# LayerNorm of the incoming unit and of the finished unit computed together, over both tiles

## What is computed

```python
x = x + _L0_conv_ref(_ln_c(x), ...)     # _ln_c: (v - mean) / sqrt(var + 1e-06), over the 512 channels
t = _to_tokens(x)
t = t + _L0_ffn_ref(_ln_t(t), ...)      # _ln_t: the same with 1e-05; the ffn replaces tokens 1..128
x = _from_tokens(t, x)
```

## Time and profile before

| | us |
|---|---|
| median of three runs | 1304.27 |
| lowest and highest | 1303.02, 1305.35 |
| profiled execution | 1302.34 |
| its span | 1300.6 |
| PE busy (matmuls) | 1100.8 (85%) |
| DVE busy | 1157.0 (89%) |
| ACT busy | 806.6 (62%) |
| POOL busy | 1110.7 (85%) |

### The profile page before, as it was taken

How to read it: one execution, slowest core, us unless ns; L and a number is a source line. 1 busy time by engine, 2 the same in 40 slices (tenths; PEclk the granted TensorE clock), 3 DMA queues, 4 the chain that set the end, 5 groups by cost and what they waited for, 6 DMA issues and landing times.

```text
span 1300.6 us, 13356 instructions
## 1 busy us (share of the span) xinstructions
PE 1100.8 (85%) x3818; PEld 660.8 (51%) x3818; DVE 1157.0 (89%) x1345; ACT 806.6 (62%) x1496; POOL 1110.7 (85%) x747
## 2 busy tenths in 40 slices
PE   6588888888888988988988988988988888887997
PEld 4344554544544544544544544545545545444887
DVE  1399999999999999999999999999999999999751
ACT  2476765766766666766666666666757657656230
POOL 4299899898898898898898898898998998988750
PEclk8789999999999898898998998999998998998998
DMA  6221321222221221221222212213212213215351
GB/s 160 75 96 53 104 97 58 87 94 77 80 98 68 92 99 57 99 99 61 98 82 78 99 64 96 99 57 104 99 56 104 99 56 116 96 63 168 115 159 30
DMA packets 64539, 116.80 MB, mean 90 GB/s; under 512 B 34218, under 2 KB 47954, under 8 KB 64466
## 3 DMA queue, kind: packets, MB, share of 16 engines
q1 hardware_dynamic: 64466, 115.96, 26.3%
HBM read 108.47 MB, written 7.47 MB: 89 GB/s over the span
## 4 chain that ended last, share of the span: by engine, by line
POOL 29%; PE 22%; DVE 21%; issue 21%; ACT 6%; POOLq 0%; SPq 0%; DVEq 0%; DMA 0%; ACTq 0%
POOL SCAN L413 16%; DVE SCAN L967 13%; PE Yp L693 8%; POOL SCAN L425 6%; DVE SCAN L922 4%; PE PP L772 3%; PE PP L839 3%; PE PP L722 2%; PE PP L819 2%; POOL XN L450 1%; PE PP L812 1%; POOL GATES L418 1%; DVE GATES L951 1%; ACT SGZ L598 1%; POOL XN L441 1%
## 5 line engine op out<-in xcount | busy, mean ns | idle before, releaser
L967 DVE TENSOR_TENSOR_SCAN SCAN<-DA,CAR,SCAN 128x384 f32<-128x384 f32 x768 | 729.8, 1000 | 38.4 <-POOL SCAN L425 36.5
L413 POOL TENSOR_TENSOR SCAN<-SCAN,CS 128x768 f32<-128x768 f32 x384 | 693.9, 1821 | 27.2 <-DVE SCAN L967 26.8
L490 ACT ACTIVATE DA<-UDT,A 128x384 f32<-128x384 f32 x768 | 441.8, 581 | 389.6 <-DVE SCAN L967 386.3
L693 PE MATMUL Yp<-SCAN,IDENT 128*128 128x384 f32 x1536 | 593.7, 512 | 97.5 <-POOL SCAN L413 89.6
L693 PEld LDWEIGHTS Yp<-SCAN,IDENT 128*128 128x128 f32 x1536 | 289.7, 198 | 304.9 <-POOL SCAN L413 143.5
L922 DVE TENSOR_TENSOR SCAN<-UDT,BB 128x768 f32<-128x768 f32 x288 | 268.7, 933 | 11.1 <-PE BB L675 9.2
L425 POOL TENSOR_TENSOR SCAN<-UDT,BS 128x768 f32<-128x768 f32 x96 | 175.4, 1827 | 0.0
L839 PE MATMUL PP<-XN,WT 128*128 128x384 f32 x384 | 139.8, 499 | 0.0
L839 PEld LDWEIGHTS PP<-XN,WT 128*128 128x128 f32 x384 | 75.8, 199 | 56.6 <-issue 11.8
L445 POOL TENSOR_TENSOR UDT<-UDT 128x768 f32<-128x768 f32 x24 | 43.5, 1811 | 69.9 <-DVE UDT L1056 69.9
L675 PE MATMUL BB<-PT,SEL 96*128 96x384 bf16 x288 | 98.3, 342 | 4.6 <-DVE SCAN L922 4.6
(11 more groups left out here) (161 smaller groups left out, 1155.4 us busy)
## 6 DMA issues: line engine op xcount, KB each, us to landing
CS<-bc_rows SPq DMA_DIRECT2D x96, 768.0 KB, 4.0
BS<-bc_rows SPq DMA_DIRECT2D x24, 768.0 KB, 6.0
out<-XN SPq DMA_DIRECT2D x32, 192.0 KB, 2.4
X<-in_x SPq DMA_DIRECT2D x24, 192.0 KB, 3.6
X<-in_L_ffn_memory_tokens SPq DMA_DIRECT2D x16, 256.0 KB, 3.0
XN<-in_L_ffn_memory_tokens SPq DMA_DIRECT2D x16, 256.0 KB, 3.1
bc_rows<-XDT SPq DMA_DIRECT2D x24, 48.0 KB, 1.5
X<-in_L_ffn_memory_router SPq DMA_DIRECT2D x1, 512.0 KB, 3.8
```

The lines of the kernel that those rows point to most:

```text
L413: pool.tensor_tensor(M[:, n1 % MRING], HB[:, n1 % HRING], over_halves(CS[:, n1 % CRING]), ALU.mult).then_inc(m_ready, 1)
L490: act.activation(DA[:, h, 0:T], DT[:, par, h], ACT.Exp, scale=A[:, h, n:n + 1])\
L693: last = pe.matmul(Yp[:, h, 0:T], IDENT[:, :], M[:, n3 % MRING, h], start=n3 == 0, stop=n3 == NS - 1)
L967: dve.tensor_tensor_scan(HB[:, s % HRING, h], DA[:, h, 0:T], HB[:, s % HRING, h], CAR[:, ds(J * NS * HALVES + s * HALVES + h, 1)], ALU.mul ...
```

## The change

`XC`, `SQ`, `LNV` and `RSTD` get a further dimension of two: index 0 is the finished unit, index 1 the incoming one. Where both exist, the mean is 4 matmuls of 192 columns over both tiles of `X` (four units apart), with the result in one bank; the subtraction, the square and the exponential are one instruction each over both. The two logarithms stay apart, since their added constants differ. POOL's instructions stay as they are, but L437 now waits for the common exponential. Where only one norm exists, the code does what it did. The pairs of semaphores become one each. The block for the mean of the finished unit now stands behind the router's matmuls in the queue, and these get a wait of their own.

```diff
-        XC = sb("XC", [P, Q, TOK]); SQ = sb("SQ", [P, Q, TOK])
-        LNV = sb("LNV", [P, TOK]); RSTD = sb("RSTD", [P, TOK])
-        XC2 = sb("XC2", [P, Q, TOK]); SQ2 = sb("SQ2", [P, Q, TOK])
-        LNV2 = sb("LNV2", [P, TOK]); RSTD2 = sb("RSTD2", [P, TOK])
+        XC = sb("XC", [P, 2, Q, TOK]); SQ = sb("SQ", [P, 2, Q, TOK])
+        LNV = sb("LNV", [P, 2, TOK]); RSTD = sb("RSTD", [P, 2, TOK])
...
-        small = SQ[:, :, :].rearrange("p q t -> p (q t)")
+        small = SQ[:, 1].rearrange("p q t -> p (q t)")
...
-        SCO = XC[0:BATCH, :, :].rearrange("p q t -> p (q t)")[:, 0:MEM]
+        SCO = XC[0:BATCH, 1].rearrange("p q t -> p (q t)")[:, 0:MEM]
...
-        STAT = PP[:, 1, 0:TOK]; STAT2 = PP[:, 0, 0:TOK]
...
+        def norms(back, norm):
+            return slice(0 if back else 1, 2 if norm else 1)
+        def norm_x(J, back, norm):
+            units = [J - 1] * back + [J + 3] * norm
+            if len(units) == 1:
+                return unit_x(units[0]).unsqueeze(1)
+            return X[:, :].rearrange("p (u q t) -> p u q t", u=UNITS, q=Q)[:, units[0]:units[1] + 1:4]
+        def norm_stat(back, norm):
+            bank = PP[:, 1 if norm else 0]
+            return bank[:, 0:(back + norm) * TOK].rearrange("p (i t) -> p i t", t=TOK)
...
                 if back and s == 13:
-                    pool.wait_ge(rstd2_ready, k + 1)
-                    pool.tensor_tensor(XC2[:, :, :], XC2[:, :, :], over_q(RSTD2[:, :]), ALU.mult)\
+                    pool.wait_ge(rstd_ready, J + 4)
+                    pool.tensor_tensor(XC[:, 0], XC[:, 0], over_q(RSTD[:, 0]), ALU.mult)\
                         .then_inc(xh2_done, 1)
...
-                    pool.wait_ge(rstd_ready, g + 1)
+                    pool.wait_ge(rstd_ready, J + 4)
                     for r1 in range(2):
-                        pool.tensor_tensor(seq_rows(unit_seq(g), r1), by_row_parity(XC[:, :, :], r1),
-                                           by_row_parity(over_q(RSTD[:, :]), r1), ALU.mult).then_inc(xn_part, 1)
+                        pool.tensor_tensor(seq_rows(unit_seq(g), r1), by_row_parity(XC[:, 1], r1),
+                                           by_row_parity(over_q(RSTD[:, 1]), r1), ALU.mult).then_inc(xn_part, 1)
...
-                if back and s == 11:
-                    act.wait_ge(xc2_ready, k + 1)
-                    act.activation(SQ2[:, :, :], XC2[:, :, :], ACT.Square).then_inc(sq2_ready, 1)
-                if back and s == 12:
-                    act.wait_ge(var2_ready, k + 1)
-                    act.activation(LNV2[:, :], STAT2, ACT.Ln, bias=EPST[:, 0:1]).then_inc(ln2_done, 1)
-                    act.wait_ge(ln2_done, k + 1)
-                    positive(act, out_ready, k)
-                    act.activation(RSTD2[:, :], LNV2[:, :], ACT.Exp, scale=-0.5).then_inc(rstd2_ready, 1)
+                if (back or norm) and s == 11:
+                    i = norms(back, norm)
+                    act.wait_ge(xc_ready, J + 4)
+                    positive(act, var_ready, J + 3)
+                    act.activation(SQ[:, i], XC[:, i], ACT.Square).then_inc(sq_ready, 1)
+                if (back or norm) and s == 12:
+                    i = norms(back, norm)
+                    stat = norm_stat(back, norm)
+                    act.wait_ge(var_ready, J + 4)
+                    if back:
+                        act.activation(LNV[:, 0], stat[:, 0], ACT.Ln, bias=EPST[:, 0:1]).then_inc(ln_done, 1 + (not norm))
+                    if norm:
+                        act.activation(LNV[:, 1], stat[:, back + norm - 1], ACT.Ln, bias=EPSC[:, 0:1]).then_inc(ln_done, 1 + (not back))
+                    act.wait_ge(ln_done, 2 * (J + 4))
+                    if back:
+                        positive(act, xh2_done, k)
+                    if norm:
+                        positive(act, xn_ready, g)
+                    act.activation(RSTD[:, i], LNV[:, i], ACT.Exp, scale=-0.5).then_inc(rstd_ready, 1)
...
-                if norm and s == 11:
-                    act.wait_ge(xc_ready, g + 1)
-                    positive(act, var_ready, g)
-                    act.activation(SQ[:, :, :], XC[:, :, :], ACT.Square).then_inc(sq_ready, 1)
-                if norm and s == 12:
-                    act.wait_ge(var_ready, g + 1)
-                    act.activation(LNV[:, :], STAT, ACT.Ln, bias=EPSC[:, 0:1]).then_inc(ln_done, 1)
-                    act.wait_ge(ln_done, g + 1)
-                    positive(act, xn_ready, g)
-                    act.activation(RSTD[:, :], LNV[:, :], ACT.Exp, scale=-0.5).then_inc(rstd_ready, 1)
...
-                if back and s == 9:
-                    pe.wait_ge(x2_ready, k + 1)
-                    if front:
-                        pe.wait_ge(relu_done, f + 1)
-                    for q in range(Q):
-                        last = pe.matmul(STAT2, MEANW[:, :], unit_x(k)[:, q], start=q == 0, stop=q == Q - 1)
-                    last.then_inc(mean2_ready, 1)
                 if at(J, ROUTE) and s == 9:
+                    pe.wait_ge(relu_done, f + 1)
...
                 if at(J, ROUTE + 1) and s == 9:
+                    pe.wait_ge(relu_done, f + 1)
                     pe.wait_ge(f_dve, 2)
...
-                    if back:
-                        pe.wait_ge(xc2_ready, k + 1)
+                    if back or norm:
+                        pe.wait_ge(xc_ready, J + 4)
                     elif front:
                         pe.wait_ge(relu_done, f + 1)
-                    if norm:
-                        pe.wait_ge(xc_ready, g + 1)
...
-                if norm and s == 9:
-                    if isinstance(g, int) and g < BATCH:
+                if (back or norm) and s == 9:
+                    if back:
+                        pe.wait_ge(x2_ready, k + 1)
+                    if norm and g < BATCH:
                         pe.wait_ge(x_first[g], 16)
-                    else:
+                    elif norm:
                         pe.wait_ge(x_loaded, 16 * (UNITS - BATCH))
                     if front:
                         pe.wait_ge(relu_done, f + 1)
-                    positive(pe, ln_done, g)
+                    positive(pe, ln_done, 2 * (J + 3))
                     for q in range(Q):
-                        last = pe.matmul(STAT, MEANW[:, :], unit_x(g)[:, q], start=q == 0, stop=q == Q - 1)
+                        last = pe.matmul(norm_stat(back, norm), MEANW[:, :], norm_x(J, back, norm)[:, :, q],
+                                         start=q == 0, stop=q == Q - 1)
                     last.then_inc(mean_ready, 1)
-                if back and s == 12:
+                if (back or norm) and s == 12:
                     if main:
                         pe.wait_ge(z_clamped, J + 1)
-                    pe.wait_ge(sq2_ready, k + 1)
+                    pe.wait_ge(sq_ready, J + 4)
                     for q in range(Q):
-                        last = pe.matmul(STAT2, MEANW[:, :], SQ2[:, q], start=q == 0, stop=q == Q - 1)
-                    last.then_inc(var2_ready, 1)
-                if norm and s == 12:
-                    if main:
-                        pe.wait_ge(z_clamped, J + 1)
-                    pe.wait_ge(sq_ready, g + 1)
-                    for q in range(Q):
-                        last = pe.matmul(STAT, MEANW[:, :], SQ[:, q], start=q == 0, stop=q == Q - 1)
+                        last = pe.matmul(norm_stat(back, norm), MEANW[:, :], SQ[:, norms(back, norm), q],
+                                         start=q == 0, stop=q == Q - 1)
                     last.then_inc(var_ready, 1)
...
-                        if back:
-                            pe.wait_ge(ln2_done, k + 1)
+                        if not norm:
+                            pe.wait_ge(ln_done, 2 * (J + 4))
...
-                if back and s == 10:
-                    dve.wait_ge(mean2_ready, k + 1)
-                    positive(dve, out_ready, k)
-                    dve.tensor_tensor(XC2[:, :, :], unit_x(k), over_q(STAT2), ALU.subtract).then_inc(xc2_ready, 1)
-                if norm and s == 10:
-                    dve.wait_ge(mean_ready, g + 1)
-                    positive(dve, xn_ready, g)
-                    dve.tensor_tensor(XC[:, :, :], unit_x(g), over_q(STAT), ALU.subtract).then_inc(xc_ready, 1)
+                if (back or norm) and s == 10:
+                    dve.wait_ge(mean_ready, J + 4)
+                    if back:
+                        positive(dve, out_ready, k)
+                    if norm:
+                        positive(dve, xn_ready, g)
+                    stat = norm_stat(back, norm)
+                    dve.tensor_tensor(XC[:, norms(back, norm)], norm_x(J, back, norm),
+                                      stat.unsqueeze(2).broadcast_to([P, back + norm, Q, TOK]), ALU.subtract)\
+                        .then_inc(xc_ready, 1)
```

(2 more changed lines are left out.)

6 lines of the change are left out of this document (2 added, 4 removed).

## The result

In 18 runs of each, the changed kernel's median is 1307.09 us and the kernel before's 1302.92 us; the ratio is 1.0026, with a 95% interval of 1.0019 to 1.0032. Measured again beside the experiments on one chip, it was 1304.57 against 1303.37 us, ratio 1.0017 (1.0007 to 1.0028). Both say slower, by 3.4 and 2.2 us going by the ratios. The profiled execution has a span of 1306.8 us, against 1300.6.

A forecast was written before the change was run, and what follows sets the result against it. It took a loop through DVE and POOL, about 49.7 us per unit, as the bound. −2.0 (subtraction) + 0.95 (router) = −1.05 us, so 1303.2 us from a median of 1304.27; range 1290 to 1308 with the rivals.

The forecast's parts named there:

- Rival A: DVE's L951 gets ahead of POOL's product: about 0.6 us less per unit, 1291.7 us; chance 0.28.
- rival B: POOL's L437 starts late and runs into DVE's L1052: 0.3 us more per unit, 1309 us; chance 0.15.
- DVE, two subtractions into one: DVE in units 1 to 20: one subtraction saves 0.10 us per unit, 2.0 us in all.
- Rival C: DVE's merged subtraction may still cost 0.94 us: +1 us, 1305.2, no change; chance 0.57 together with the forecast.
- ACT, two squares into one: ACT: L516 starts 0.10 us earlier, worth nothing while L951 stands behind POOL's product.
- PE, eight records instead of sixteen: PE at steps 9 and 12: half the matmuls, twice the columns; hidden or not waited for, worth zero.
- The shared RSTD: POOL's L437 waits for one exponential over both tiles: cost 0, at most 0.15 us per unit.
- PE in the units with the router: Unit 22: router's matmuls now precede the mean, which DVE awaits: 0.95 us more, once; unit 21 in time.
- The loop: Each unit's path: DVE from 528.55 to 534.1, POOL to 542.09, DVE to 546.7, POOL to the next unit.
- DVE waiting for the mean at step 10: Sign in the next profile by which the forecast would be wrong as a whole; no size given.

The follow-up runs named there:

- e7: e1 with the one subtraction split again into one for each tile; 1301.48 us (one run), units 49.67 us apart.
- e8: e1 with the one square split into two, all else merged; 1300.41 us (one run), units 49.60 us apart.
- e6: e1 with POOL's clamp of SGZ moved behind its product and DVE's first gate combine; 1293.45 us, ratio 0.9928 to the kernel before.
- e3: Changed kernel with the mean put back ahead of the combine's matmuls in unit 23, left behind the router's in unit 22; 1303.51 us, ratio 1.0006.
- e4: e1 with the gate's square on ACT put ahead of the LayerNorm square; 1293.93 us, ratio 0.9933 to the kernel before.
- e1: Changed kernel with the mean put back ahead of the router's and the combine's matmuls, all merging kept; 1302.0 us, ratio 0.9993.
- e5: Kernel before, nothing merged, with POOL's clamp of SGZ moved behind its product and DVE's first gate combine; 1288.31 us, ratio 0.9894.
- e9: e6 with squares, their sums, logarithms and exponentials per tile again, finished unit first; 1288.34 us, ratio 0.9892 to the kernel before.

## Why the prediction was wrong

Forecast was 1303.2 us and no change that can be told; it came out slower, by 0.17 to 0.26%. The 1307.09 us lie inside the range of 1290 to 1308, but that was made wide for rivals A and B, and neither of them is what happened. By the prediction's own steps:

- **DVE, two subtractions into one:** right in kind, a little large. 0.10 us per unit were forecast and 0.07 came; e7 gives them back exactly. The step of the merged instruction is 0.86 us where L922's 0.84 was taken, and that of the second single one 0.46 where 0.47 was. Rival C, that the merged subtraction is no cheaper, is answered with this.
- **ACT, two squares into one:** right. No time (e8), and the arrival 0.03 us behind POOL's product is what the trace shows.
- **PE, eight records instead of sixteen:** right. At 541.58 the sums of the squares took 2.48 us for eight records (2.56 and a tail were taken); over the 20 units it was 1.54 to 2.90 us with the clock, and nothing in the loop waited for PE.
- **The shared RSTD and rival B:** right for this kernel. L437's place was forecast 3.3 us after the combine and came at 2.87 to 3.36, up to 0.79 us later than before, where 0.65 was named as the most; L1053 took 0.93 us all the same. Its mechanism is real, as e6 shows, but it needs a shorter loop to cost anything.
- **PE in the units with the router:** here it failed. The step read "Swapped, the mean ends at about 1176.2, and DVE asks for it at 1175.25: 0.95 us more, once." For unit 22 that was good: e3 measured 0.87 us. But the block moved past two things, and the step counted one. The matmuls of the combine, which the same queue holds at step 9 of unit 23, were left out, so their price stood in the sum as nothing. It is 2.1 us by the profiles, more than all that the change wins. They stood in the code (`COMBINE` has an entry for step 9 of unit 23, and the diff takes the mean from above that loop to below it), and the trace of before had them at 1241.94 us. With this term and the measured gain the sum is −1.3 + 0.9 + 2.1 = +1.7 us. The two ratios say 2.2 and 3.4 us. The rest is of the size of what the clock did in single profiles (0.9 to 1.4 us at the start of unit 23, 2 to 3 us at unit 1), but no run separates it.
- **Rival A:** not met, as was likelier, but its place and mechanism were right and its price near. Where e4 makes DVE come first, it gains 0.49 us per unit against e1 (49.60 − 49.11), where 0.58 were forecast.
- **The loop:** right, as far as these runs try it. e5, e6 and e9 were built on it and shorten it by 0.4 to 0.7 us per unit.

The chance of 0.15 for slower was all rival B's. The mechanism that made it slower was not among the rivals. One sign of it was named, DVE waiting for the mean at step 10, and it is what the trace shows, 4.71 us in unit 23; but it was named for the steady units, with no look at what unit 23 has on PE.

## What to carry to other kernels

When a diff moves a block in an engine's queue, list what it moves past in every unit or iteration, the special ones at the end too, and price each one on the engine that bounds that stretch; the steady part of a program tells nothing about it. A merged instruction waits for the later of its inputs and serves the earlier of its readers later: that is free only while the reader has cover, and the cover is the first thing that the next improvement takes. And look for an instruction of known shape that takes nearly three times as long as its twin: moving 0.8 us out of the run it stood behind was worth ten times the merging.
